# Low half of B by accumulating transfers, low products of the first output inside the fourth z, and the fifth tile's convolution by three products

## The reference, cut to what matters

```python
# x (32, 64, 1024), 4 groups of 16 channels, 9 taps; ctx from cond and its weights
h = conv1d(x, weight, groups=4, pad=4) + ctx[:, :, None] + bias[None, :, None]
q = h @ Wq_w.T                       # 16 wide
scores = q @ keys.T                  # 64 experts
gate = softmax over the 16 largest scores, 0 elsewhere
z = (h @ A_w.T).reshape(..., 64, 8) * gate[..., None]    # 512 wide
out = x + 2 * (z.reshape(..., 512) @ B_w.T)
```

## Time and profile before

| | us |
|---|---|
| runs of the kernel | 234.87, 235.16, 235.43 (median 235.16) |
| the profiled execution | 235.88 |
| its span, from the first to the last instruction | 234.1 |
| PE busy | 230.0 (98% of the span) |
| DVE busy | 192.4 (82%) |
| ACT busy | 99.4 (42%) |
| POOL busy | 1.5 (1%) |
| DMA, mean rate | 163 GB/s |

### The profile page before, as it was taken

One profiled execution on the slowest core, in us unless ns is written; L12 is line 12 of the kernel. 1 busy time (PEld: TensorE's weight loads), 2 busy tenths in 40 slices (PEclk: granted clock), 3 DMA queues, 4 the chain that ended last, 5 costly groups with the idle time before them and its releaser, 6 DMA issues.

```text
span 234.1 us, 4016 instructions
## 1 busy us (share of the span) xinstructions
PE 230.0 (98%) x1387; PEld 205.2 (88%) x1387; DVE 192.4 (82%) x465; ACT 99.4 (42%) x246; POOL 1.5 (1%) x10
## 2 busy tenths in 40 slices
PE   8999999999999999999999999999999999999995
PEld 8988998798988989898898989889898988989884
DVE  2699899999969899898999889898988977846522
ACT  3899757356253263524425352532535241202100
POOL 2000000000000000000000000000000000000000
PEclk9999999999999999999999999999999999999999
DMA  6999045653534728264372726446281352716222
GB/s 202 377 406 383 16 128 176 222 162 126 173 146 109 239 77 244 98 161 158 101 260 66 254 88 163 155 114 246 66 280 58 70 193 54 230 45 224 92 90 90
DMA packets 22916, 38.26 MB, mean 163 GB/s; under 512 B 2544, under 2 KB 11120, under 8 KB 22896
## 3 DMA queue, kind: packets, MB, share of 16 engines
q1 hardware_dynamic: 22752, 37.89, 49.0%
q10 hardware_dynamic: 144, 0.12, 0.2%
HBM read 25.68 MB, written 12.32 MB: 162 GB/s over the span
## 4 chain that ended last, share of the span: by engine, by line
PE 90%; ACT 5%; DMA 2%; SPq 1%; issue 1%; DVE 0%; ACTq 0%
PE p_z L644 35%; PE p_out L689 13%; PE p_out L690 13%; PE p_out L697 13%; PE p_conv L598 10%; ACT h_c L393 3%; PE p_out L644 3%; PE p_conv L541 3%; DMA x_blk<-in_x_blocks 2%; ACT a_hi L357 1%; ACT x_hi L357 1%; PE p_z L673 1%; ACT h_hi L357 0%; SPq L279 0%; PE p_t L656 0%
## 5 line engine op out<-in xcount | busy, mean ns | idle before, releaser
L689 PE MATMUL p_out<-b_hi,zt_hi 128*128 128x512 f32 (+1 forms) x128 | 50.2, 393 | 0.0
L690 PE MATMUL p_out<-b_hi,zt_lo 128*128 128x512 f32 (+1 forms) x128 | 50.1, 392 | 0.0
L697 PE MATMUL p_out<-b_lo,zt_hi 128*128 128x512 f32 (+1 forms) x128 | 34.4, 391 | 0.0
L644 PE MATMUL p_z<-a_hi,h_lo 128*128 128x264 f32 x240 | 34.2, 285 | 0.0
L644 PE MATMUL p_z<-a_hi,h_hi 128*128 128x264 f32 x240 | 34.1, 285 | 0.0
L644 PE MATMUL p_z<-a_lo,h_hi 128*128 128x264 f32 x240 | 34.0, 284 | 0.0
L644 PEld LDWEIGHTS p_z<-a_hi,h_hi 128*128 128x128 f32 x240 | 32.0, 188 | 1.6 <-issue 0.4
L644 PEld LDWEIGHTS p_z<-a_hi,h_lo 128*128 128x128 f32 x240 | 31.2, 188 | 0.0
L644 PEld LDWEIGHTS p_z<-a_lo,h_hi 128*128 128x128 f32 x240 | 31.0, 188 | 0.0
L357 ACT ACTIVATE h_hi<-h_t 128x1024 fp32r<-128x1024 f32 x16 | 17.1, 1066 | 31.9 <-DVE h_t L805 31.9
L690 PEld LDWEIGHTS p_out<-b_hi,zt_lo 128*128 128x128 f32 x128 | 24.0, 188 | 5.6
(11 more groups left out here) (109 smaller groups left out, 267.7 us busy)
## 6 DMA issues: line engine op xcount, KB each, us to landing
x_nat<-in_x_rows SPq DMA_DIRECT2D x16, 512.0 KB, 5.2
out_dram<-x_nat SPq DMA_DIRECT2D x31, 256.0 KB, 2.3
x_blk<-in_x_blocks SPq DMA_DIRECT2D x14, 516.0 KB, 3.9
z_dram<-a_raw SPq DMA_DIRECT2D x60, 64.0 KB, 1.8
a_raw<-z_dram SPq DMA_DIRECT2D x15, 256.0 KB, 3.7
a_raw<-in_a_wq SPq DMA_DIRECT2D x8, 264.0 KB, 7.1
x_nat<-in_b_w SPq DMA_DIRECT2D x4, 512.0 KB, 10.0
x_blk<-in_x_blocks SPq DMA_DIRECT2D x2, 258.0 KB, 4.1
```

Source lines behind the costliest of these rows:

```text
L644: mm = nc.tensor.matmul(z_bank(t, b)[:, 0:HB], h[:, t % 2, r, :], a[:, r, b * HB:(b + 1) * HB], start=k == 0 and r == 0, stop=k == 2 and r ...
L689: nc.tensor.matmul(dst, zt_hi[:, t % 2, c, :], b_hi[:, c, cols], start=c == 0, stop=False)
L690: nc.tensor.matmul(dst, zt_lo[:, t % 2, c, :], b_hi[:, c, cols], start=False, stop=False)
L697: mm = nc.tensor.matmul(dst, zt_hi[:, t % 2, c, :], b_lo[:, c, start:stop], start=False, stop=c == JC - 1)
```

## The change

1. **B's low half.** ACT writes `b_lo[c] = -b_raw[c]` with the same rounding as `b_hi` (`negate_b`), and POOL issues a transfer of `b_raw[c]` into `b_lo[c]` that adds to what is there (`accum_op=ALU.add`). DVE's four subtractions go. `s_blo` becomes one semaphore per chunk, which PE and `load_rows` wait for.
2. **The first output.** `out_high(0, *)` stays; `out_low(0, 0)` and `out_low(0, 1)` move into z(3), behind 40 of its 48 matmuls.
3. **The fifth tile.** `TW` is 4: tile 4 goes by `conv_sum` and `conv_pair`, nine matmuls in place of twelve, with the additional work on DVE and ACT that tiles 5 to 15 have.
4. **The keys.** The small operands come by two transfers: 164 columns first, the last 65 columns (the keys' high copy and a mask) later on SP's queue. `split_keys` moves from before `add_u(0, 0)` to after `split_h(4)` on ACT, and into tile 3 on DVE.
5. **The orders** of ACT and DVE for tiles 1 to 4 are written anew around these.

```diff
-TW = 5
+TW = 4
...
                 else:
-                    sp.wait_ge(s_blo, t + 1)
+                    sp.wait_ge(s_blo[t], 16)
                 sp.dma_start(x_nat[:, t % XN, :], x_rows[t]).then_inc(s_xn[t % XN], 16)
...
             load_blocks(3)
+            sp.dma_start(sm[:, SMALL_KH:SMALL], small[:, SMALL_KH:SMALL]).then_inc(s_keys, 16)
             sp.dma_start(w_raw[:, 1], conv_w[:, 1]).then_inc(s_w[1], 16)
...
+            for c in range(JC):
+                pool.wait_ge(s_bneg, c + 1)
+                pool.dma_start(b_lo[:, c, :].bitcast(F32), b_raw[:, c, :], accum_op=ALU.add).then_inc(s_blo[c], 16)
...
+            def negate_b(c):
+                nc.scalar.activation(b_lo[:, c, :], b_raw[:, c, :], ACT.Copy, scale=-1.0).then_inc(s_bneg, 1)
...
             def split_keys():
-                act.wait_ge(s_small, 16)
+                act.wait_ge(s_keys, 16)
...
-            act.dma_start(sm[:], small).then_inc(s_small, 16)
+            act.dma_start(sm[:, 0:SMALL_KH], small[:, 0:SMALL_KH]).then_inc(s_small, 16)
             split_w(0)
             split_x(0, 0)
             split_x(0, 1)
             split_x(1, 0)
             split_x(1, 1)
-            split_keys()
             add_u(0, 0)
...
             split_h(2)
-            split_x(4)
+            split_b(0)
+            negate_b(0)
             take_q(1)
             split_w(1)
             copy_q(1)
-            split_b(0)
+            split_x(4)
+            sum_w(1)
+            take_q(2)
             split_b(1)
-            take_q(2)
             exp(1)
             copy_q(2)
-            split_h(3)
-            split_z(0)
             split_b(2)
             split_b(3)
-            add_u(4)
+            split_z(0)
+            split_h(3)
+            negate_b(1)
+            negate_b(2)
             exp(2)
-            sum_w(1)
+            negate_b(3)
+            add_u_shared(4)
             split_x(5)
             take_q(3)
             split_z(1)
             split_h(4)
+            split_keys()
...
             scores(2)
-            conv(4)
+            conv_sum(4)
+            conv_pair(4)
             out_high(0, 0)
             out_high(0, 1)
-            out_low(0, 0)
-            out_low(0, 1)
             for i in range(3, NT):
                 for k in range(3):
                     z_product(i, k, (1,), range(R))
                 z_product(i, 0, (0,), range(R))
                 z_product(i, 1, (0,), range(R))
+                if i == 3:
+                    out_low(0, 0)
+                    out_low(0, 1)
...
-            def split_b(c):
-                dve.wait_ge(s_bhi, c + 1)
-                low(b_lo[:, c, :], b_raw[:, c, :], b_hi[:, c, :], s_blo)
...
             split_h(2)
-            split_x(4)
+            differ(4, 0)
+            differ(4, 1)
             turn_h(3, 0)
             turn_h(3, 1)
+            sum_w(1)
             split_w(1)
...
```

More of the change, by code:

```diff
@@ L143, in adaln_ffn @@
         s_small = sem("s_small")
+        s_keys = sem("s_keys")
         s_st = [sem(f"s_st{k}") for k in range(XN)]
@@ L163, in adaln_ffn @@
         s_bhi = sem("s_bhi")
-        s_blo = sem("s_blo")
+        s_blo = [sem(f"s_blo{c}") for c in range(JC)]
+        s_bneg = sem("s_bneg")
         s_cw = sem("s_cw")
@@ L695, in out_low @@
                     if t == 0 and k == 0:
-                        pe.wait_ge(s_blo, c + 1)
+                        pe.wait_ge(s_blo[c], 16)
                     mm = nc.tensor.matmul(dst, zt_hi[:, t % 2, c, :], b_lo[:, c, start:stop], start=False, stop=c == JC - 1)
@@ L969, in _ @@
             top_first(1)
-            split_b(0)
+            split_x(4)
             take_first(1)
             top_second(1)
-            split_b(1)
+            split_ws(1)
             take_second(1)
@@ L978, in _ @@
             turn_z(1)
-            split_z(0)
-            split_h(3)
             copy_scores(2)
             top_first(2)
-            split_b(2)
+            split_z(0)
             take_first(2)
             top_second(2)
-            split_b(3)
             take_second(2)
+            split_h(3)
             weigh(2)
@@ L990, in _ @@
             gate(2)
-            sum_w(1)
+            turn_z(2)
             differ(5, 0)
             differ(5, 1)
-            split_ws(1)
-            turn_z(2)
+            add_shared(4, 0)
+            add_shared(4, 1)
             turn_h(4, 0)
@@ L999, in _ @@
             split_z(1)
+            add(0, 0)
             split_h(4)
-            add(0, 0)
+            add(0, 1)
             for i in range(3, NT):
@@ L1013, in _ @@
                     split_z(i - 1)
-                if i + 2 < NT:
+                if 3 < i < NT - 2:
                     add(i - 3, 1)
```

## The result

The changed kernel took 239.87 us (median of 5 runs, 239.37 to 240.51) against 235.16 us before; the ratio is 1.020 (95% interval 1.019 to 1.022). Forecast were 234.6 us in a range of 233.8 to 236.4. It is slower by 4.7 us.

The account below looks back on a forecast made before the run. PE, busy 230.0 of 234.1 us, was taken as the bound: its list plus its stands. Less 0.37 (start), plus 0.05 (first output), less 0.22 (old stand) gave 235.16 - 0.54 = 234.6 us, range 233.8 to 236.4.

Parts of the forecast that it names:

- the price of a chunk: Adding transfers of b_lo before z(3)'s low products: 2.0 us per chunk, the last landing at 48.4, just in time.
- prediction's own formula: Landing of the last b_lo chunk: negation end 40.14, fixed 1.65, z(1)'s return 0.65, three chunks at r; needed by 48.7.
- turning point of 2.1: At z(3)'s low products: the price in us per chunk at which the last b_lo chunk lands at 48.7, when needed.
- A term put at nothing: DMA at 44 to 49 us: the 1.5 MB of x rows wait for the chunks and so cost them nothing.
- The rival at three passes: Inside z(3): additions at 3.84 us per chunk, PE waiting 5.3 us, 239.9 us in all; near three passes some 12%.
- The three matmuls fewer: conv(4) and first output: 0.70 us shorter, but PE waits for DVE's zt_lo, losing that and 0.05 us more.
- Gate(2): DVE before z(3): gate(2) ends at 43.0, ready for PE at 43.15, so z(3) follows the high products without a stand.
- The old stand of 0.22 us: PE between the first output's high products and z(3)'s second group, behind gate(2) on DVE; to go, gaining 0.22 us.
- The start: Before conv(3): keys moved (0.30 us) and a smaller first transfer (0.07) shorten ACT's list; 0.37 us gained, bounds 0 and 0.53.
- Slow transfers: Inside z(3): PE waits for b_lo because adding is slow; 236.0 us at double cost, 239.9 at three passes; chance 28%.
- DVE not holding PE: At the first output: zt_lo comes 0.75 us sooner than counted, so all 1.29 us are gained, 233.9 us; chance 11%.
- No shorter start: Behind 9 us: arriving transfers pace ACT, so the start stays and 0.1 to 0.2 us are left, 235.0; chance 15%.

Follow-up runs that it names:

- rows_late: The changed kernel with the loads of x rows for tiles 1 to 3 held until all four chunks of B were added; median 237.08 us, ratio 1.010.
- plain: The changed kernel with the four GpSimd transfers copying B into b_lo without adding, so only its times count; span 232.7 us, one execution of 234.53 us.
- fill: The changed kernel with fifteen unused 128-column matmuls of ones ahead of the first low product; median 238.07 us, ratio 1.013.
- tw5: The changed kernel with earlier negations of chunks 1 and 2, and the fifth tile's convolution back at twelve matmuls; median 234.90 us, ratio 0.999.
- neg_early: The changed kernel with ACT's negations of chunks 1 and 2 earlier and z(0)'s high half ahead of B's last; median 235.44 us, ratio 1.002.

## Why the prediction was wrong

*The step that failed* is the price of a chunk: "I take 2.0, between the cheap end and double". It was 3.0 us of all 16 engines, where a plain copy on the same queue took 1.45. That is twice a copy; the forecast's "double" of 2.56 was too low because its single price, 1.28 from the rate of other transfers, was. With the prediction's own formula, 40.14 + 1.65 + 0.65 + 3r, 3.0 gives 51.4, or 51.0 in an execution that ran 0.45 ahead. Measured were 51.86, and 50.8 in rows_late, without the loads of rows. The price of "double" was in the text with its consequence and 28% of the chance; for a value just below the turning point of 2.1 no row spoke.

*A term put at nothing.* The prediction said that the rows of x "don't stand in their way". But `load_rows(1)` waits only for chunk 1 and was issued at 45.20, while the last two chunks were still under way. In the changed kernel that is 1.0 us (rows_late). It weighs on plain copies too: with r = 1.45 the formula gives 46.8, or 46.0 in plain's execution (conv(3) 0.76 ahead), and the last copy landed at 47.99. No run separates the loads there, but a copy at the cheapest price would hardly have landed at the forecast's 45.2.

*The price of waiting was also wrong.* Each rival took a wait of PE at its length. The wait was 51.88 - 48.49 = 3.4 us; then the stretch from the fourth low product to the paired convolution took 4.74 us (51.88 to 56.62) instead of 3.09 (48.20 to 51.29 in plain) while the granted clock read 0.63 from 52 to 56, in part of it the lower level of 1.2 GHz (the products of the convolution come every 0.42 us from 55.19 to 56.04, instead of 0.234): 1.65 us. 3.39 + 1.65 - 0.13 = 4.91, the difference of the distances; the 0.13 are the 0.11 that plain shows as gained, and 0.02 ahead of the low products. fill and the spread of rows_late's runs show the second term without the first.

*Why the sum of a rival came out all the same.* The rival at three passes had r = 3.84 and a wait of 5.3 us, and named 239.9. Measured were r = 3.0 and a wait of 3.4, and the clock's 1.65 made up most of the rest. That is luck: the rival's mechanism, a slow addition, is right, its number is not.

*The three matmuls fewer*: right. PE went to the first output at 39.12, 0.7 us behind the end of the convolution. The profile names no releaser there, but `zt_hi` was ready at 37.78 and `zt_lo` ended at 39.01, so it was `zt_lo`, as worked out. z(3) stood 22.16 us after conv(3), forecast 43.34 - 21.21 = 22.13. tw5 shows that the shorter convolution alone gives nothing: VectorE's additional rows swallow it. The first chunk did not slow z(0)'s trip: ACT went on to `zt_hi` at 37.16, straight behind B's high halves.

*Gate(2)*: right; z(3) follows the high products without a stand (the sixteenth begins at 42.69, z(3) at 42.92), gate(2) ends at 42.47 (forecast 43.0, this execution being 0.45 us earlier). The old stand of 0.22 us is gone.

*The start*: 0.37 us forecast, conv(3) came 0.82 earlier in the profile, but the runs made to measure it give 0.25 (interval from 0.6 less to nothing) and none. The mechanism, ACT's list, is right only in part: where the blocks of x come early, conv(0) on PE paces ACT and the keys stand in a gap.

*Sum*: of 0.54 us forecast without the transfers, plain's distance shows 0.11, where the forecast's own (0.54 less 0.37 at the start) is 0.17.

*The rivals.* Slow transfers: right in kind, at twice a copy's price, with a load of rows and the clock on top. DVE not holding PE: fell. No shorter start: neither shown nor excluded. The fit in the Trainium skill, page "DMA: Bandwidth & Descriptors", section "Anatomy of one DMA — SWDGE (gpsimd) path", gives 3.2 us for 512 KB, by which chunk 3 would have landed at 45.5. It holds for plain copies here at best (3.1 us the quickest landing, 4.0 the median, 6.2 the last); for transfers that add the shortest was 5.2.

No version here beats the kernel before beyond its interval. What stays open: why an addition holds the engines twice as long as a copy, since no run shows what they do meanwhile, and what decides whether a wait of 2 to 3 us lowers the clock. The mean clock was 0.993 in one of four runs of rows_late and 1.000 in the other three; in all five of the changed kernel it was 0.984 to 0.993.

## What to carry to other kernels

A transfer that adds is not free because an idle engine issues it: here it held all DMA engines twice as long as a copy of its bytes, and other work that goes by DMA paid too (z(1)'s trip to DRAM, 7.2 us instead of 3.1 in neg_early). When a forecast hangs on the price of an operation that no row shows, and the turning point lies between its bounds, do not take the value just beside it; measure that operation alone, or say that both sides are equally likely. And shortening the list of the busiest engine pays only where nobody else ends last: look at who it waits for next, and price a wait with the clock that it may cost.

## What the runs showed of the hardware

- An adding transfer of 512 KB inside on-chip memory, issued by GpSimd: 3.0 us of 16 engines; landing 5.2 us after issue when alone, 9.7 as the third in a row beside loads of rows. The same as a copy: 1.45 us, landing after 3.1 to 6.2 us.
- TensorE's granted clock: after 3.4 us of standing it read 0.63 over 52 to 56 us, and the work there took 1.65 us longer; with matmuls on ones in the gap it stayed 1.00 and the median was 1.8 us lower.
- GpSimd's subtraction of 128 x 1024 took 2.34 to 3.14 us and held VectorE's subtractions beside it (1.22 to 3.41 us, 0.28 to 1.82). The Trainium skill, page "SBUF — State Buffer", section "Who interferes with whom", says that VectorE's tensor_tensor with both inputs in SBUF contends with GpSimd's reads; the trace agrees: VectorE's, begun 0.08 us behind GpSimd's at 28.67, ended 1.1 us behind its end.
- The start varies from execution to execution: in the eleven programs with the same start conv(3) began anywhere from 20.45 to 21.14 us.
